# The last layernorm of a graph kernel: centring moved to TensorE, squares to ScalarE, scaling and the affine pass to VectorE

## The reference, cut to what matters

```python
def _layernorm(x, axis=-1, eps=1e-05):
    m = jnp.mean(x, axis=axis, keepdims=True)
    v = jnp.var(x, axis=axis, keepdims=True)
    return (x - m) / jnp.sqrt(v + eps)
...
    # _L1_gnn_ref, its end; out is [6250, 128]
    mean = out.mean(axis=0)
    var = out.var(axis=0)
    y = (out - mean) * jax.lax.rsqrt(var + BN_EPS) * gamma + beta
    return jnp.where(y >= 0, y, ALPHA * y)      # ALPHA = 0.01
...
    x = _layernorm(x + _L1_gnn_ref(x, edge_index, ...), axis=-1)
    return x
```

## Time and profile before

| | |
|---|---|
| median of 3 runs | 987.84 us (987.67 to 988.26) |
| the profiled execution | 989.45 us |
| its span, first to last instruction | 987.6 us |
| outside of its span | 1.85 us |
| mean granted TensorE clock | 0.986 of full speed |
| `finish_rows`, from VectorE's first instruction | 947.04 us to the end of the span, 40.6 us |

### The profile page before, as it was taken

The page is one execution under the profiler, slowest core; times in us unless marked ns, Lnnn a source line. Parts: engine busy times, 40 slices in busy tenths (PEclk is TensorE's granted clock), DMA queues, the critical chain, the costliest instruction groups (busy, mean ns, idle before and its releaser), DMA issues. The chain is left out here.

```text
span 987.6 us, 31422 instructions
## 1 busy us (share of the span) xinstructions
PE 905.9 (92%) x12418; PEld 809.5 (82%) x12418; DVE 692.1 (70%) x1690; ACT 466.2 (47%) x944; POOL 367.1 (37%) x492
## 2 busy tenths in 40 slices
PE   1479999999999999999999999999999999999955
PEld 0367888888988888888898888899988888888855
DVE  5997999999989888889888879888722111112256
ACT  0645666666566565556565556565532000000037
POOL 4554476667544434334434334424212110111000
PEclk9989999999999999999999999999999999999978
DMA  5558988888788778677668677668563977788334
GB/s 164 199 201 290 359 303 333 299 303 316 268 270 297 250 266 291 226 243 234 215 223 281 213 249 235 223 220 279 173 257 132 399 277 292 257 307 323 112 114 150
DMA packets 95685, 247.94 MB, mean 251 GB/s; under 512 B 41128, under 2 KB 63356, under 8 KB 89644
## 3 DMA queue, kind: packets, MB, share of 16 engines
q1 hardware_dynamic: 93132, 240.97, 69.0%
q0 software_dynamic: 2400, 4.88, 1.6%
HBM read 185.46 MB, written 60.35 MB: 249 GB/s over the span
## 5 line engine op out<-in xcount | busy, mean ns | idle before, releaser
L952 ACT CAST counts<-pair_ps 128x800 bf16<-128x800 f32 x391 | 319.0, 829 | 282.5 <-PE pair_ps L771 278.9
L549 DVE TENSOR_TENSOR lo_oh<-counter,lo_t 128x1024 bf16<-128x1024 bf16 x391 | 273.7, 700 | 83.4 <-PE pair_ps L771 80.5
L789 PE MATMUL x_ps<-counts,xsplit 128*128 128x256 bf16 (+1 forms) x2500 | 315.9, 271 | 5.5 <-issue 4.5
L789 PEld LDWEIGHTS x_ps<-counts,xsplit 128*128 128x128 f16 x2500 | 226.8, 98 | 39.6 <-issue 17.4
L771 PE MATMUL pair_ps<-key_oh,lo_oh 128*128 128x100 bf16 x3128 | 208.1, 210 | 27.2 <-DVE key_oh L552 19.3
L552 DVE TENSOR_TENSOR key_oh<-counter,key_t 128x800 bf16<-128x800 bf16 x391 | 232.4, 594 | 0.0
L771 PEld LDWEIGHTS pair_ps<-key_oh,lo_oh 128*128 128x128 bf16 x3128 | 182.3, 98 | 44.8 <-DVE key_oh L552 25.8
L808 PE MATMUL e_ps<-streams 128*32 128x128 f32 x3528 | 109.4, 278 | 0.2 <-issue 0.2
L797 PE MATMUL x_ps<-counts,zown 128*128 128x256 bf16 (+1 forms) x840 | 103.3, 269 | 0.0
L857 PE MATMUL pair_ps<-streams,zown 128*128 128x256 bf16 x904 | 101.8, 273 | 0.0
L808 PEld LDWEIGHTS e_ps<-streams 128*32 128x32 f32 x3528 | 95.6, 112 | 5.5 <-issue 1.1
(11 more groups left out here) (158 smaller groups left out, 925.5 us busy)
## 6 DMA issues: line engine op xcount, KB each, us to landing
streams<-in_edge_attr SPq DMA_DIRECT2D x196, 576.0 KB
counts_kept<-counts SPq DMA_DIRECT2D x10, 1664.0 KB, 8.5
streams<-counts_kept SPq DMA_DIRECT2D x6, 1664.0 KB, 6.6
counts<-counts_kept SPq DMA_DIRECT2D x4, 1664.0 KB, 6.6
counts_kept<-counts SPq DMA_DIRECT2D x2, 3200.0 KB, 12.7
streams<-counts_kept SPq DMA_DIRECT2D x2, 3200.0 KB, 15.6
dinv_row<-dinv_rows SPq DMA_DIRECT2D x25, 128.0 KB, 5.5
edst<-in_dst SPq DMA_DIRECT2D x196, 4.5 KB
```

Of the source, the lines that this page charges most:

```text
L549: dv.tensor_tensor(lo_oh[:, at % RING, :, :, :], counter[:, :, :].unsqueeze(1).to_broadcast([P, SW // 2, P, 2]), pairs(lo_t[b % 2][:, w]). ...
L789: last = nc.tensor.matmul(x_ps[:, 0, 0:n], xsplit[:, q // 2, q % 2, :], by_hi[:, q // 2, :], start=(q == 0), stop=(q == 2 * HI - 1))
L952: a.copy(out.rearrange("p h (g n) -> p h g n", g=2), pair_ps[at % 2][:, :, 0:4 * KW].rearrange("p g (n h) -> p h g n", h=HI)).then_inc(S[" ...
```

## The change

- Rows are centred by TensorE. The matmul of L1243 no longer multiplies by the identity but by `center`, the identity minus 1/128. A VectorE memset (`eps`) and a VectorE subtraction (`center`) come ahead of everything else in this piece. The transposed `r` loses its row mean in this way. `x1` is itself the output of a layernorm, so its rows have mean zero already.
- With centred rows the variance is the mean of squares. ScalarE squares each tile from PSUM and sums it in the same call (`ACT.Square` with `accum_out`). The squares themselves go to `xo`, which is overwritten later. ScalarE then takes the root of sum/128 + eps in one instruction for the chunk.
- VectorE makes the reciprocal and then scales the whole chunk with one `tensor_tensor` from PSUM, the scale broadcast along the features.
- Batch normalisation moves from ScalarE to VectorE, just ahead of `leaky`.
- bn_stats, bn_aggr, the addition of epsilon, the shift, and ScalarE's `normalise` go away.

```diff
+        center, eps = sb("center", [P, F], F32), sb("eps", [P, 1], F32)
...
-            def batch_norm(c):
-                a, z = CHUNKS[c]
-                reach(act, r_ready, c - RB + 1)
-                nc.scalar.activation(t[c % RB][:, 0:BN * (z - a)], y[:, a * BN:z * BN], ACT.Identity,
-                                     bias=co[:, 2:3], scale=co[:, 1:2]).then_inc(t_ready, 1)
-
-            def take_root(c):
-                act.wait_ge(var_ready, c + 1)
-                nc.scalar.activation(std[c % 2][:, 0:size(c)], std[c % 2][:, 0:size(c)], ACT.Sqrt).then_inc(std_ready, 1)
-
-            def normalise(c):
-                act.wait_ge(scales_ready, c + 1)
+
+            def row_stds(c):
+                act.wait_ge(turned, c + 1)
                 reach(act, kept[c % XB], 16 * (c // XB))
+                reach(act, xo_ready, c - 1)
                 for i in range(size(c)):
-                    last = nc.scalar.activation(xo[c % XB][:, i * F:(i + 1) * F], v_ps[c % VB][:, i, :], ACT.Identity,
-                                                bias=shift[c % 2][:, i:i + 1], scale=std[c % 2][:, i:i + 1])
-                last.then_inc(xo_ready, 1)
...
+                    last = nc.scalar.activation(xo[c % XB][:, i * F:(i + 1) * F], v_ps[c % VB][:, i, :], ACT.Square,
+                                                accum_out=std[c % 2][:, i:i + 1])
+                last.then_inc(squared, 1)
+                act.wait_ge(squared, c + 1)
+                nc.scalar.activation(std[c % 2][:, 0:size(c)], std[c % 2][:, 0:size(c)], ACT.Sqrt, bias=eps[:, 0:1],
+                                     scale=1.0 / F).then_inc(std_ready, 1)
+
+            act.wait_ge(center_ready, 1)
+            for c in range(LC + 1):
+                row_stds(c)
...
+            vv.memset(eps[:, :], LN_EPS).then_inc(center_ready, 1)
+            vv.tensor_scalar(center[:, :], ident[:, :], 1.0 / F, None, ALU.subtract).then_inc(center_ready, 1)
...
-            def row_stats(c):
...
-                for i in range(k):
-                    last = vv.bn_stats(lstats[e][:, i, :], v_ps[c % VB][:, i, :])
...
-                for i in range(k):
-                    last = vv.bn_aggr(lmv[e][:, i, :], lstats[e][:, i, :])
...
+            def batch_norm(c):
+                a, z = CHUNKS[c]
+                reach(dve, r_ready, c - RB + 1)
+                vv.tensor_scalar(t[c % RB][:, 0:BN * (z - a)], y[:, a * BN:z * BN], co[:, 1:2], co[:, 2:3],
+                                 ALU.mult, ALU.add).then_inc(t_ready, 1)
...
+            def row_scales(c):
+                k = size(c)
+                dve.wait_ge(std_ready, c + 1)
+                if c == LC - XB:
+                    dve.wait_ge(turned, c + 1)
+                    vv.memset(x1[LC % XB][:, 0:2 * F], 0.0).then_inc(x1_cleared, 1)
+                nstep(vv.reciprocal(std[c % 2][:, 0:k], std[c % 2][:, 0:k]))
+                vv.tensor_tensor(xo[c % XB][:, 0:k * F].rearrange("p (i f) -> p i f", f=F), v_ps[c % VB][:, 0:k, :],
+                                 std[c % 2][:, 0:k].unsqueeze(2).to_broadcast([P, k, F]), ALU.mult).then_inc(xo_ready, 1)
+
             for c in range(LC + 3):
                 if c <= LC:
+                    batch_norm(c)
                     leaky(c)
                 if c >= 2:
                     row_scales(c - 2)
-                if 1 <= c <= LC + 1:
-                    row_stats(c - 1)
...
+            pe.wait_ge(center_ready, 2)
...
-                    nc.tensor.matmul(v_ps[c % VB][:, i, :], r[c % RB][:, base + i % 2:base + BN:2], ident[:, :],
+                    nc.tensor.matmul(v_ps[c % VB][:, i, :], r[c % RB][:, base + i % 2:base + BN:2], center[:, :],
```

More of the change, by code:

```diff
@@ L1112, in finish_rows @@
         x1, xo = ([sb(f"{n}{i}", [P, C * F], F32) for i in range(XB)] for n in ("x1_", "xo"))
-        lstats = [sb(f"lstats{i}", [P, C, 6], F32) for i in range(2)]
-        lmv = [sb(f"lmv{i}", [P, C, 2], F32) for i in range(2)]
-        std, shift = ([sb(f"{n}{i}", [P, C], F32) for i in range(2)] for n in ("std", "shift"))
+        center, eps = sb("center", [P, F], F32), sb("eps", [P, 1], F32)
+        std = [sb(f"std{i}", [P, C], F32) for i in range(2)]
         v_ps = [ctx.enter_context(nc.psum_tensor(f"u1_vps{i}", [P, C, F], F32)) for i in range(VB)]
-        pre, root, coeff, norm = sem("pre_step"), sem("batch_root"), sem("coefficients"), sem("norm_step")
-        t_ready, r_ready, turned, var_ready, std_ready = sem("t_ready"), sem("r_ready"), sem("turned"), sem("var_ready"), sem("std_ready")
-        scales_ready, xo_ready, x1_cleared = sem("scales_ready"), sem("xo_ready"), sem("x1_cleared")
+        pre, root, norm = sem("pre_step"), sem("batch_root"), sem("norm_step")
+        t_ready, r_ready, turned, squared, std_ready = sem("t_ready"), sem("r_ready"), sem("turned"), sem("squared"), sem("std_ready")
+        center_ready, xo_ready, x1_cleared = sem("center_ready"), sem("xo_ready"), sem("x1_cleared")
         x1_in, kept = ([sem(f"{n}{i}") for i in range(XB)] for n in ("x1_in", "kept"))
@@ L1155, in _ @@
             nc.scalar.activation(co[:, 0:1], co[:, 0:1], ACT.Sqrt).then_inc(root, 1)
-            act.wait_ge(coeff, 1)
-            def batch_norm(c):
-                a, z = CHUNKS[c]
-                reach(act, r_ready, c - RB + 1)
-                nc.scalar.activation(t[c % RB][:, 0:BN * (z - a)], y[:, a * BN:z * BN], ACT.Identity,
-                                     bias=co[:, 2:3], scale=co[:, 1:2]).then_inc(t_ready, 1)
-            def take_root(c):
-                act.wait_ge(var_ready, c + 1)
-                nc.scalar.activation(std[c % 2][:, 0:size(c)], std[c % 2][:, 0:size(c)], ACT.Sqrt).then_inc(std_ready, 1)
-            def normalise(c):
-                act.wait_ge(scales_ready, c + 1)
+            def row_stds(c):
+                act.wait_ge(turned, c + 1)
                 reach(act, kept[c % XB], 16 * (c // XB))
+                reach(act, xo_ready, c - 1)
                 for i in range(size(c)):
-                    last = nc.scalar.activation(xo[c % XB][:, i * F:(i + 1) * F], v_ps[c % VB][:, i, :], ACT.Identity,
-                                                bias=shift[c % 2][:, i:i + 1], scale=std[c % 2][:, i:i + 1])
-                last.then_inc(xo_ready, 1)
[L1176 to L1181, removed]
-                if 1 <= c <= LC + 1:
-                    take_root(c - 1)
+                    last = nc.scalar.activation(xo[c % XB][:, i * F:(i + 1) * F], v_ps[c % VB][:, i, :], ACT.Square,
[7 more added lines that the diff above has]
+                row_stds(c)
         @block.vector
@@ L1196, in _ @@
             pstep(vv.tensor_tensor(co[:, 2:3], vec[:, 2:3], co[:, 3:4], ALU.subtract))
-            dve.sem_inc(coeff, 1)
-            def row_stats(c):
[L1200 to L1203, removed]
-                for i in range(k):
-                    last = vv.bn_stats(lstats[e][:, i, :], v_ps[c % VB][:, i, :])
-                nstep(last)
-                reach(dve, xo_ready, c - 1)
-                for i in range(k):
-                    last = vv.bn_aggr(lmv[e][:, i, :], lstats[e][:, i, :])
[L1210 to L1218, removed]
+            def batch_norm(c):
[3 more added lines that the diff above has]
+                                 ALU.mult, ALU.add).then_inc(t_ready, 1)
             def leaky(c):
```

## The result

The changed kernel takes 980.7 us (979.83 to 985.3, 10 runs) against 987.48 us (984.98 to 988.26, 10 runs) for the kernel before beside it. The ratio is 0.9947, 95% interval 0.9933 to 0.996: faster by about 5.2 us, half a per cent. In the third of the four jobs one run of the kernel before took 3245 us and one of before_bn_dve 1354 us, and these two are left out of the ratios.

A forecast was written before the change was run, and what follows sets the result against it. The late last load behind chunk 4's store was taken to bound the end: 976.5 + 1.19 + 1.7 + 4.35 = 983.75, a 3.85 us gain, so 987.84 - 3.85 = 984.0 us, range 982.3 to 986.6.

The forecast's parts named there:

- this chain: Chunk 4's turn, statistics and scaling, its store, the last load's 5.5 us landing, two tiles, last store set the end.
- Start: Before the first chunk: VectorE gains 0.2 us of setup, batch normalisation gets shorter; TensorE starts at 950.2, not 950.35.
- Rival A: ScalarE's squares become the bound if slow per tile; break-even 0.49 us; chance 0.07 within 0.2%, 0.06 slower.
- B: ScalarE reloads its function table between Square and Sqrt, at least +10 us; chance almost nothing.
- The doubt about batch normalisation: On VectorE, 1024 columns take 0.8 us, at most 1.33; costs nothing, as VectorE waits for chunk 4's root anyway.
- The gate: Chunk 4's store and the last load behind it: turned-to-scaled lag 4.55 us, before 7.05; load issued 3.1 us earlier.
- The landing: Last `x1` load, from issue to TensorE's start on the last chunk: unchanged at 5.55 us.
- Rival C: Chunk 5's store collides with the last load, 1.6 us; median 985.6, or 987.5 with later scaling; chance 0.13.
- D: Last load lands in 3.8 us, like a 256 KB one; median about 982.3; chance 0.08.
- The last two tiles and the store: After TensorE's last start: 1.19 us matmuls, 1.7 normalising (0.8 less than before), 4.35 for the unchanged store.
- How the numbers follow: Closing step giving chances and range: faster 0.82, same 0.12, slower 0.06; 8 in 10 within 982.3 to 986.6.

The follow-up runs named there:

- before_bn_dve: Only batch normalisation moved from ScalarE to VectorE, against the kernel before: ratio 1.0033 (1.002 to 1.0046).
- before_tail_early: Last chunk's residual rows given their own buffer and loaded behind the first four loads, against the kernel before: ratio 0.9991 (0.9982 to 1.0).
- before_again: No edit, the kernel before run against itself: ratio 1.0001 (0.9988 to 1.0013).
- after_norm_act: Changed kernel with the scaling put back on ScalarE, one instruction for each tile: ratio to the kernel before 1.0051 (1.0032 to 1.007).
- after_warm: Changed kernel with seven identity matmuls added on TensorE ahead of the first chunk: 972.22 us, ratio to the kernel before 0.997 (0.9958 to 0.9981).

## Why the prediction was right or wrong

**What bounds the kernel.** Half right. The late last load was on the path: TensorE's idle moved with it and went when it was loaded early. But "the end is set by this chain" was too strong for the kernel before: before_tail_early shows ScalarE's queue within about 0.9 us of it. The forecast did not suffer, because the change took work off both; that was luck as far as the reasoning went, since the forecast had asked only about the load.

**Start.** The forecast let TensorE start 0.15 us earlier. It started 0.06 us earlier in the first profile and 0.2 later in the second, where its own branch held it.

**ScalarE.** Squares stand 0.25 us apart in place of 0.30, the root starts 2.21 us after the first square (956.29 to 958.50). Rival A, with a break-even of 0.49, is refuted. No table load appears in the last part, so B is too.

**VectorE.** Batch normalisation 0.804 (forecast 0.8), scaling 1.224 (1.23). The doubt about batch normalisation was said to cost nothing, and in the changed kernel VectorE indeed waits 0.72 us for the root ahead of chunk 4's scaling.

**The gate.** Chunk 4 is turned at 963.65 and scaled at 967.86: 4.2 us, forecast 4.55, before 7.05. The load is issued, relative to TensorE's start, 21.77, 20.32 and 21.20 us later in the three profiles, forecast 20.75. The spread is the clock at the start: the sum took the 3.4 us at half clock of one profile as given, where the runs show 3.3 to 6.1. The term was mis-sized by up to 1.4 us for that. My estimate, with half of the slow stretch beyond 3.4 us taken out: 20.4, 20.4 and 20.7 us, so the work itself was forecast within 0.4.

**The landing.** 5.43, 5.89 and 5.74 us, forecast 5.55. Rival C's full collision (1.6 us) did not come, and D's 3.8 us did not either.

**The last two tiles and the store.** 7.17 to 7.19 us, forecast 7.25. The gain against the kernel before is larger than the 0.8 said when its last chunk falls back to half clock (8.90).

**The total.** In sum the changed piece takes 37.3 us on average where 36.7 was forecast, and the gain over the mean of two profiles before is 3.9, forecast 3.85. The two later comparisons, 0.996 and 0.9964, are at the forecast (984.0 / 987.84 = 0.9961). That 3.9 meets 3.85 so closely is partly luck: the changed piece takes 0.6 more than forecast, and the kernel before takes 0.6 more on the mean of two profiles than in the one that the forecast used.

**The step that failed** is "How the numbers follow": the range. It was made from the doubts in the changed piece alone (start, hops and landing, D, C) and held the 947 us ahead of it to the value of one profile, so the scatter of that part stood in it at nothing. The same paragraph puts 2 us to what a measurement can tell from no change, and used them for the chances only. What the runs showed: in the profile of the changed kernel the last part begins 3.7 us earlier than in the one before, and its ten runs span 979.83 to 985.3, 5.5 us, while the last part differs by 0.7 us among its three profiles. The median came 3.3 us below the forecast although the changed piece itself took 0.6 more than forecast. (The upper end of the range, 986.6, is called the full C, but C's own figures are 985.6 and 987.5.) The first comparison shows 5.2 us of gain, 1.3 more than the changed piece gives. Whether that rest is scatter alone is not shown for that chip, since no second comparison was made there; the interval of 0.9933 to 0.996 just reaches the 0.996 of the second.

## What to carry to other kernels

When a chain of short steps between two engines seems to set the end, look at what a third engine is idle for, and then at how late the queues of the first two are without that wait. Here TensorE waited for a load, that load and ScalarE's queue were within about a microsecond, and only an edit that shortened both paid. Moving work to an engine is worth what the order allows it; batch normalisation on ScalarE lost the whole gain one chunk ahead and, by the ratios, some 1.5 us of it two chunks ahead, which is within the scatter of that job. A small transfer over an awkward number of partitions can be slow (here 53 KB over 53 partitions, 4.34 us to the end; cut into 48 and 5, 2.35), so try to cut it where it stands last. And a range for a small gain has to hold the scatter of the untouched part, not only the doubts about the touched one.

## What was not expected of the hardware

- The same program takes 987.5, 975.1, 975.1 and 988.6 us (medians of the kernel before) in the four jobs. Between the two profiles of it the last part begins at 947.04 and 932.32. In three of the jobs its runs span 3.3, 5.1 and 8.3 us.
- TensorE's clock comes back to full 3.3 to 6.1 us after its first matmul behind 10.8 to 11.3 us of idle, in profiles of the same kernel. Ahead of the last chunk it fell to half in an idle of 3.46 us (before_again) and of 4.67 (after_norm_act), while after 3.70 us of idle that chunk ran at full clock. After 3.28 us (before_bn_dve) it began at full clock and fell within its first 0.3 us.
- In after_warm TensorE came out of its branch 3.15 us after VectorE had begun the last part.
- A DMA of 53 partitions moved at some 20 GB/s (23 in the earlier trace rows, 18 for the last store of the changed kernel); cut into 48 and 5, the span ended 2 us earlier after the issue.
